# A graph-attention edge loop: GpSimd's gathers wait for the gather two back

## What is computed

```python
def _gatv2(x, edge_index, edge_attr, W_l, b_l, W_r, b_r, W_e, att, bias):
    x_l = (x @ W_l.T + b_l).reshape(n, HEADS, DIMS)
    x_r = (x @ W_r.T + b_r).reshape(n, HEADS, DIMS)
    ...
    s = x_l[src] + x_r[dst] + e_feat
    s = jax.nn.leaky_relu(s, NEG_SLOPE)
    alpha = jnp.einsum('ehc,hc->eh', s, att)
    amax = jax.ops.segment_max(alpha, dst, num_segments=n)
    ex = jnp.exp(alpha - amax[dst])
    denom = jax.ops.segment_sum(ex, dst, num_segments=n)
    alpha = ex / (denom[dst] + 1e-16)
    out = jax.ops.segment_sum(alpha[..., None] * x_l[src], dst, num_segments=n)
    return out.reshape(n, FEAT) + bias
```

## Time and profile before

| | us |
|---|---|
| median of 3 runs | 3181.06 |
| lowest and highest of them | 3168.73 and 3182.11 |
| the profiled execution: span from the first to the last instruction | 3452.9 |
| busy in it: PE, DVE, ACT, POOL | 3048.3, 1834.2, 1508.7, 1189.9 |

### The profile page before, as it was taken

The page is one execution under the profiler, slowest core; times in us unless marked ns, Lnnn a source line. Parts: engine busy times, 40 slices in busy tenths (PEclk is TensorE's granted clock), DMA queues, the critical chain, the costliest instruction groups (busy, mean ns, idle before and its releaser), DMA issues. The chain is left out here.

```text
span 3452.9 us, 50836 instructions
## 1 busy us (share of the span) xinstructions
PE 3048.3 (88%) x13612; PEld 2420.6 (70%) x13613; DVE 1834.2 (53%) x3643; ACT 1508.7 (44%) x4936; POOL 1189.9 (34%) x1152
## 2 busy tenths in 40 slices
PE   6678888788888888884999999999999999999999
PEld 5456656566565665563778877877787888888898
DVE  5566666666676666676754564374365435111103
ACT  2067666777667676775322322232231212222232
POOL 4556555565555655630310031030021001222210
PEclk9899899999999999997999999999999988999999
DMA  7556655555665655554211011100001032333361
GB/s 217 152 148 148 145 145 141 143 144 141 149 145 145 147 142 150 136 94 124 52 38 37 27 30 31 41 8 1 15 27 50 1 100 84 128 120 119 119 176 38
DMA packets 288628, 345.06 MB, mean 100 GB/s; under 512 B 155176, under 2 KB 213655, under 8 KB 284512
## 3 DMA queue, kind: packets, MB, share of 16 engines
q1 hardware_dynamic: 232813, 174.79, 19.1%
q0 software_dynamic: 53632, 157.89, 17.6%
q10 hardware_dynamic: 2064, 10.81, 1.0%
HBM read 298.03 MB, written 44.37 MB: 99 GB/s over the span
## 5 line engine op out<-in xcount | busy, mean ns | idle before, releaser
L1470 POOL DMA_INDIRECT a_g<-xl_d,a_ix x480 | 468.1, 975 | 311.6 <-issue 116.0
L1504 PE MATMUL b_pM<-b_m,b_oh 128*112 128x281 f32 x1680 | 513.6, 451 | 28.5 <-DVE g_acc L1644 22.5
L1599 ACT ACTIVATE b_m<-a_g,c_pcx 128x64 f32<-128x64 f32 x1856 | 460.4, 334 | 33.6 <-issue 33.6
L1504 PEld LDWEIGHTS b_pM<-b_m,b_oh 128*112 128x112 f32 x1680 | 327.6, 200 | 156.7 <-issue 69.0
L1470 POOL DMA_INDIRECT XS<-xl_d,a_ix x344 | 333.3, 969 | 216.5 <-issue 91.1
L1637 DVE SCALAR_TENSOR_TENSOR a_r<-a_pS,g_attx 128x528 f32<-128x528 f32 x420 | 286.6, 699 | 198.4 <-remote 91.6
L1599 ACT ACTIVATE b_m<-XS,c_pcx 128x64 f32<-128x64 f32 x1424 | 351.5, 333 | 14.3 <-issue 14.2
L2286 ACT ACTIVATE f_hid<-f_pH,f_b 128x256 f32<-128x256 f32 (+3 forms) x360 | 161.9, 451 | 423.0 <-PE f_pH L2180 409.9
L450 PE MATMUL m_pH<-m_h,m_w 128*128 128x313 f32 (+1 forms) x1280 | 342.3, 426 | 4.5 <-DVE m_h L612 4.5
L125 POOL TENSOR_TENSOR m_rstd<-m_ve,m_mhalf 125x5 f32<-125x5 f32 x41 | 48.0, 1170 | 801.5 <-DVE m_ve L111 801.5
L1497 PE MATMUL a_pS<-g_xr,a_lt 128*128 x840 | 237.1, 406 | 97.8 <-ACT a_pS L1581 60.8
(11 more groups left out here) (413 smaller groups left out, 4629.2 us busy)
## 6 DMA issues: line engine op xcount, KB each, us to landing
a_db<-dl_d SPq DMA_DIRECT2D x212, 224.0 KB
f_w<-in_ffn_W1p SPq DMA_DIRECT2D x16, 1024.0 KB
wide_w<-in_ffn_W1p SPq DMA_DIRECT2D x16, 1024.0 KB
m_w<-in_mix_W SPq DMA_DIRECT2D x8, 1024.0 KB
f_w<-in_ffn_W2p SPq DMA_DIRECT2D x8, 1024.0 KB
a_g<-xl_d,a_ix POOLq DMA_INDIRECT x480
a_lt<-eat_d SPq DMA_DIRECT2D x214, 32.0 KB
eat_d<-a_stage SPq DMA_DIRECT2D x15, 448.0 KB
```

Source lines behind the costliest of these rows:

```text
L1470: p.indirect_dma_start(out=gathered(t)[:, j, :], out_offset=None, in_=xl_d, in_offset=bass.IndirectOffsetOnAxis(ap=IX[:, t // BSTEPS, n:n ...
L1504: ins = pe.matmul(pM[0:WN, h, 0:MW], OH[:, b, j, :], M[:, b, j, :], start=(j == 2 * h), stop=(j == 2 * h + 1))
L1599: ins = a.activation(m[:, j, part], gathered(ts)[:, j, part], ACT.Copy, scale=of[:, first + j, h, 0:1])
```

## The change

The edge loop gets four semaphores, `a_h0` to `a_h3`, one for each of a step's four gathers, in place of the 14 of the ring slots. `landed(i, t)` is the value that such a semaphore has when gather j of step t in round i has landed. Ahead of each gather GpSimd waits for one of them: gathers 0 and 1 for gathers 2 and 3 of the step before, gathers 2 and 3 for gathers 0 and 1 of the same step. The first two gathers of the loop are exempt. PE waits for gathers 0 and 1 alone ahead of its first scores, ACT for gathers 2 and 3 ahead of its copy. No computation changes.

```diff
--- before.py
+++ after.py
@@ -1357,9 +1357,9 @@
 
                     return isinstance(i, int) and i == 0
 
-                def rows_landed(i, t):
-
-                    return 64 * i if t < EARLY else 64 * i + 64
+                def landed(i, t):
+
+                    return 16 * RING * i + 16 * (t + 1 - EARLY)
 
                 def chain_of(i, t):
 
@@ -1467,8 +1467,11 @@
                             if j % 2 == 0:
                                 wait(p, f"a_scored{j // 2}", base, t + 1 - AHEAD)
                                 p.sem_inc(s["a_seen"], 1)
+                            if not (at_start(i) and t == EARLY and j < 2):
+                                p.wait_ge(s[f"a_h{(j + 2) % IG}"], landed(i, t - (1 if j < 2 else 0)))
+                                p.sem_inc(s["a_seen"], 1)
                             p.indirect_dma_start(out=gathered(t)[:, j, :], out_offset=None, in_=xl_d,
-                                                 in_offset=bass.IndirectOffsetOnAxis(ap=IX[:, t // BSTEPS, n:n + 1], axis=0)).then_inc(s[f"a_g{t}"], 16)
+                                                 in_offset=bass.IndirectOffsetOnAxis(ap=IX[:, t // BSTEPS, n:n + 1], axis=0)).then_inc(s[f"a_h{j}"], 16)
 
                     rounds(p, slot)
 
@@ -1511,7 +1514,8 @@
                             wait(pe, "a_onehot", base, t + 1)
                             pe.wait_ge(s[f"a_eat{t % LTS}"], 32 * i + 16 * (t // LTS) + 16)
                             if not (at_start(i) and t < EARLY):
-                                pe.wait_ge(s[f"a_g{t}"], rows_landed(i, t))
+                                for j in (0, 1):
+                                    pe.wait_ge(s[f"a_h{j}"], landed(i, t))
                             scores_of_first(ws)
 
                         if tau == 0:
@@ -1576,7 +1580,8 @@
                         par = 1 if odd else 0
                         if exists(base, t, 0):
                             if not (at_start(i) and t < EARLY):
-                                a.wait_ge(s[f"a_g{t}"], rows_landed(i, t))
+                                for j in (2, 3):
+                                    a.wait_ge(s[f"a_h{j}"], landed(i, t))
                             wait(a, "a_gated1", base, t)
                             a.activation(pS[0:TE, 2:4, 0:GD], gathered(t)[:, 2:4, :], ACT.Copy).then_inc(s["a_filled"], 1)
                         if tau == 3:
```

## The result

The changed kernel takes 3794.51 us (median of 4 runs, 3786.36 to 3795.1) beside 3180.36 us for the kernel before on the same chip: a ratio of 1.194 (95% interval 1.191 to 1.197), 614 us slower. The profiled execution took 3786.36 us with a span of 3784.6.

The account below looks back on a forecast made before the run. Latency and hand-overs between engines bound the edge loop, POOL close below. With POOL's waits, 206 steps of 7.0 us (1442) plus 70 for staging make 1512 against 1119 us: +393, 3574 us; range 3220 to 3700 us.

Parts of the forecast that it names:

- A: Likeliest case: POOL bound in the edge loop, holes in the profile alone; 3574 us, range 3286 to 3714; chance 0.66.
- What bounds the loop: Edge loop: bound by latency and hand-overs between engines, POOL not far below, needing 5.0 us of each 6.75 us step.
- holes: Edge-loop stretches where engines start nothing new until the last gather lands; one beside staging gathers was 6.32 us long.
- The 272 us between the profile and the median: Profiled span exceeds timed median by 271.8 us; booked mostly to profile-only holes, so the timed loop is 1119 us.
- rival B: Holes real in timed runs too, the timed loop already 1391 us; +121 us, 3302 us, or +39, 3220; chance 0.14.
- (1) The pair: POOL's new waits: landing 2.6 plus wake-up 0.9 make a pair of gathers 3.5 us, was 2.5; steps 7.0 us.
- (2) What lands late: Gathers queued behind 2 MB of staging land late; POOL waits out 4.7 us a round, 70 us over 15 rounds.
- (3) Finer waits of PE and ACT: PE and ACT wait for two semaphores instead of one: costed at nothing, 21 us if POOL did not bind.
- (4) POOL's extra instructions: POOL's sem_inc and wait instructions, four a step: costed at nothing, 82 us if their cover is gone.
- (5) Holes gone: Fewer gathers in flight remove the holes: time back in the profiled frame, nothing on top with POOL the bound.
- the row of 2.5 to 2.9 us: Profile row bounding one gather's landing: DMA engines empty after 2.5 us, other engines saw its end after 2.93 us.
- The signs named ahead of time: Changed trace: gather pairs 3.5 us apart, landings ending POOL's idle, even 7.0 us steps, no holes, span near median.

Follow-up runs that it names:

- e16: The kernel before, unchanged, run and traced again on a chip where before took 3169.0 us: 3173.3 us, ratio 1.002.
- e6: The kernel before, unchanged, run and profiled again on a chip where before took 3438.82 us: 3437.07 us, ratio 1.000.
- e5: The changed kernel itself, run again beside a kernel before of 3438.82 us: 3809.68 us, ratio 1.108.
- e9: The changed kernel with line 1384's broadcast of destination nodes cut to 16 partitions from 112, result not the layer's: 3702.79 us, ratio 1.078.
- e4: The changed kernel without POOL's waits, each pair of gathers with its own semaphore, PE's and ACT's split waits kept: 3436.56 us, ratio 1.000.
- e7: The changed kernel with POOL's waits kept, but PE and ACT waiting for all four gathers of a step: 3816.8 us, ratio 1.109.
- e1: The changed kernel with each gather waiting for the one just before it, one in flight instead of two: 5213.59 us, ratio 1.516.
- e14: The kernel before with a 128x768 float memset on POOL ahead of each gather, no landing waits: 3650.31 us, ratio 1.148.
- e8: The changed kernel with line 1434's load of edge attributes made for one item instead of four: 3797.05 us, ratio 1.104.
- e2: The changed kernel with each gather waiting for the one three back instead of two: 3492.65 us, ratio 1.015.
- e3: The changed kernel with each gather waiting for the one four back instead of two: 3481.51 us, ratio 1.013.
- e10: The kernel before with line 1384's broadcast of destination nodes cut to 16 partitions from 112, result not the layer's: 3435.44 us, ratio 1.001.
- e11: The kernel before with the gathers' lead (AHEAD) cut from three steps to two: 3470.0 us, ratio 1.011.
- e12: The kernel before with a 128x4 float memset on POOL ahead of each gather, no landing waits: 3452.58 us, ratio 1.005.

## Why the prediction was wrong

The direction, the engine and the mechanism were right; the loss was 393 us in the prediction and 614 on the chip, and the measured 3794.51 us lie 94 us above the range's high end. Nearest comes the far end of A's own range, 3714 us; no other rival is nearer. Its steps, in order:

- **What bounds the loop.** "Latency and hand-overs, with POOL not far below" was read from an execution with holes. Without them it is POOL's issue that binds (e16).
- **The 272 us between the profile and the median.** The size was right: the prediction set the timed loop at 1119 us, and e16 shows 1113.9. The cause was wrong. The holes don't belong to profiled executions but to some executions on some chips, timed ones included (e6). Where they are present, the change costs less, for it takes them away: 371 us in e5, at almost the same absolute time (3809.68 and 3794.51 us). This is rival B's mechanism; it gave 121 us there, short for the reason that follows.
- **(1) The pair.** Right: 3.5 us expected, 3.56 found. Over 412 pairs 0.06 us make 25 us. In part this was luck: the landing was put at 2.6 us and is 2.8, the wake-up at 0.9 us and is 0.78.
- **(2) What lands late. This is the step that failed.** It counted 70 us, for the gathers behind staging alone. The trace has 277 us over the 1465 that 823 starts at 1.78 us take: 91 us in the staging steps (14 times 13.60 - 7.12), 53 in the steps with the stores (15 times 10.67 - 7.12), and 133 over the other steps (176 times 0.75). A staging step costs 6.5 us where the sum had 4.7. The sum took the two staging gathers' own issue off the 7.2 us of their data; but this issue is time in the loop too (in e16 the staging step is 3.15 us longer), which would explain the difference, though no run tests it. e9's loop is 99 us shorter than the changed kernel's, so about that much of the 277 comes with the broadcast of the destination nodes, 77 us of it in the other steps. SP's traffic was in no term: the prediction took one landing of 2.6 us, next to a hole in which the last gather had the DMA engines to itself, for all 824. Together: 25 + 21 (91 against 70) + 53 + 133 = 232 us, about the 230 that lie between 1512 and 1742.4 us. That the 53 us come from the stores is argued from their place alone, since no run leaves them out, and the remaining 56 us of the other steps are put down to no transfer.
- **(3) Finer waits of PE and ACT.** Nothing, as predicted (e4, e7).
- **(4) POOL's extra instructions.** Nothing, as predicted: where the awaited landing has long come, the gap is still 0.30 us (the gather at 1047.26 us).
- **(5) Holes gone.** Right: none in the changed trace. In the timed comparison of the result that is worth nothing, as predicted, since the timed executions of before had none to lose (their level is e16's). In e5 the loss is 243 us smaller (614 - 371) because the kernel before had them.

The Trainium skill (DMA: Bandwidth & Descriptors, section Anatomy of one DMA — SWDGE (gpsimd) path) gives an estimate of 2.3 us for a gather of this size. The landing measured is 2.7 us at least and 2.8 in the median (e1, e14), so the row of 2.5 to 2.9 us was the better guide, and the measurement decides.

The signs named ahead of time held: starts 3.57 us apart two by two, landings as releasers in 446 of 824 cases, holes gone, span within 10 us of the median. Steps "near 7.0 us and alike" didn't hold: twelve of a round's steps have a mean of 7.87 us, the other two 10.67 and 13.60. Nor did PE wait for gathers in most steps: ACT did, 205 times, PE 20 times. One reading of the prediction was off without weight in the sum: POOL is at four to six tenths in the first 17 slices, and at three in the 18th.

**What stays open.** What makes the holes. On the chips where before has them they come with three or more gathers on their way (two or one: 0 to 8 groups in e1, e5, e7, e8 and e9; three, four or unbounded: 105 to 125 in e2, e3, e4, e6, e10, e11 and e12), and other executions have none at the same pace. Whether the pace or the number counts there, and what differs between the chips, no run tells.

## What to carry to other kernels

A bound on how many transfers are on their way turns a latency into a rate: it costs nothing only while landing plus wake-up, divided by the number allowed, stays below the issuing engine's own pace (here 3.56/n against 1.25 us), and even then late landings are waited for (57 us with three, 46 with four). So price such a wait with the landings as they are beside the other queues' traffic, step by step of a round, not with one taken while the DMA engines were idle. And where a profile's span differs from the timed median, have the unchanged kernel traced again before the difference is booked to the profiler.

## What the runs showed of the hardware

- An indirect gather of 128 rows of 1056 bytes lands 2.7 us after its start at least, 2.8 in the median and 6.7 at most in e1, although only one beside the staging gathers was on its way; POOL's next one starts 0.78 us after the landing.
- Traffic of another queue delays a gather's landing: with 224 KB a step cut to a seventh, the changed kernel's twelve ordinary steps went from a mean of 7.87 us to 7.43 (e9). With 2 MB ahead on its own queue the step takes 6.5 us more than two undisturbed pairs (13.60 against 7.12).
- The kernel before has two levels, 3169 to 3181 and 3432 to 3439 us, on different chips, with and without some hundred moments at which waiting engines are released late (118 in e6, none in e16). The changed kernel, with at most two gathers on their way, took 3794.51 us beside the one level and 3809.68 beside the other.
- The mean granted clock of TensorE in the loop was 0.99 of 2.4 GHz in e16, where PE was busy for 93% of it, and 0.86 in the changed kernel, where PE was busy for 73%; PE's busy time for nearly the same instructions went from 1032.92 to 1272.90 us. The loss doesn't come through this clock: POOL's gathers waited 9.9 us for PE in the whole changed loop, and 747.5 us for landings.
